# Layer norms by exp(-ln/2) and a rebuilt routed stage in a hybrid conv, attention and routed network: what it does to the time

## The chip, the cores and the metric

The kernel runs on one core of one Trainium2 chip. The metric is the device time of one launch in microseconds (us), the median of three runs. Besides the runs, one execution was taken with the hardware profiler; its trace holds every instruction with its start and length. Engines: PE is TensorE (PEld its weight loads), DVE is VectorE, ACT is ScalarE, SP is the queue that issues the DMAs. A name with q (SPq, DVEq) is the sequencer of an engine, which runs register loads, branches and waits.

## The reference

The input is 16 sequences of 256 positions with 32 channels, f32. Five blocks follow each other, each added to the residual `X`:

```python
# norm over the 32 channels ahead of each block: (x - mean) / sqrt(var + 1e-5)
# L0: recurrence over the 256 positions, state = tanh(A state + input), out = C state + D skip
# L1: group norm, three 1x1 projections with prelu, softmax(q k) v over positions
# L2: causal attention, 4 heads, rope, LoRA on q, k, v; then a linear, batch statistics and
#     a second recurrence over 256 positions, state = sigmoid(V state + input)
# L3: a two-direction Mamba-like scan (decays exp(segment sums), silu gates, RMS norm each way)
# last, a routed network: 33 blocks x 19 operations
op = argmax(h[0, 0, :19])               # of the first token, before the first step and after each
# block i acts if attn_mask[i, op] or ffn_mask[i, op]; ffn is relu(h w1 + b1) w2 + b2
```

A block that has neither mask set for the picked operation is skipped. With the given data the kernel before executes two feed-forward steps and no attention step of the routed network (the profile shows 2 sets of the feed-forward's DMAs and none of the attention's).

## The kernel before

Channels and a group of 4 sequences lie on the 128 partitions, 4 x 256 positions on the free axis, so a full tensor is 128 x 1024 and its halves 128 x 512 fill one PSUM bank each. Each engine has its own instruction list, written out by hand; they meet only in named semaphores (`then_inc`, `wait_ge`). An engine works strictly through its list. `link(...)` in DVE's list makes the next DVE instruction wait for this one.

A **norm** (`norm_tensor`, `norm_vector`, `norm_scalar`, used five times) runs so: PE multiplies by the centring matrix (L234, two halves); ACT squares (L270) and DVE copies the centred values (L253); PE sums squares with the data as the stationary side, so that a variance lies by token (L238, 8 small products); ACT takes the square root (L274), DVE the reciprocal (L257) and spreads it over 32 columns (L259); PE turns it back (L244, 8 products); DVE multiplies (L264). ACT loads the table of the square root ahead of each (L267).

The two **recurrences** (`recur_tensor`, `recur_scalar`) are 256 steps each, in which a small PE product (L314) and one ACT function (L332) wait for each other. The inputs of 32 steps lie in one PSUM bank; in the first recurrence DVE must add a bias to a bank (`bias_bank`, L1042) before step 32k of it can start. PE writes the input products of bank k+1 between steps 17 and 26 of bank k. Between `bias_bank(1)` and the loop that does `bias_bank(2)` DVE's list holds the making of the routing table `acting` (L1054 to L1060): for each of 33 blocks and 19 operations, the next block that acts. It is a chain of 33 pairs of linked 19-element operations.

The **Mamba block** has 48 units in each direction: exp on ACT (L985), a product on DVE (L1287), PE around them, and every 12 units a gate on DVE (L343, L346). In the second direction DVE also normalises the first one's result, one quarter every 12 units: a reciprocal of 128 x 256 (L1308), two short operations (L1309, L1310). At the end the same is done for the second direction in two halves of 128 x 512 (L1316, L1318, L1319).

The **routed stage** (`routed`) runs on all engines at once. Each engine has its own registers for the block and the operation; it loads the operation (L397, L419), then `acting` (L398, L421), then the two masks (L404, L405), and branches. In a feed-forward step SP issues four DMAs (L459 w1; L463 to L465 b1, w2, b2). w1 lies 4 times on the partitions; DVE spreads it into four matrices with zeros (`w1z`, L1375), PE multiplies (L837, 8 products of 128 rows), ACT and DVE take the relu in turn (L1017, L1390), PE the second layer on four column strips at once (L846), DVE adds the bias (L1381). Only then does `pick` read the first token out of the result for the next operation (L1329 to L1337). The three nested loops have 36 turns; those left over are run through as empty ones (L424). Then DVE adds `xn` to `X` (L1397) and SP stores it.

## Time and profile before

| what | value |
|---|---|
| median of 3 runs | 739.93 us (739.02 to 740.48) |
| the profiled execution's own time | 742.2 us |
| its span, first to last instruction | 740.4 us |
| two recurrences, first to last step | 27.4 to 157.9, and 362.4 to 506.0 |
| last norm finished, routed stage begins | 688.4 |
| routed stage, up to the last write of its result | 688.4 to 729.8 |
| loops left, last add and store | 729.8 to 740.4 |
| busy share of PE, DVE, ACT | 71%, 46%, 45% |

All times in the text are in us from the span's start, unless marked otherwise. In rows of the timeline the first number is the start, the second the busy time of the group, xN the number of instructions merged, and the bracket the engine's idle time before it with what ended it. An f32 product appears as two PE instructions.

### The profile page before, as it was taken

Reading aid. Unit: us, or ns where it says so; the run is one execution under the profiler, and the core shown is the slowest. Engines: PE = TensorE matmul, PEld = TensorE weight load, DVE = VectorE, ACT = ScalarE, POOL = GpSimd, SP = SyncE. Lnnn points to the kernel's source line nnn. Section 1 sums busy time; section 2 is a strip of 40 time slices with the busy share of each in tenths; the row PEclk is TensorE's granted clock in tenths of the full one; section 3 lists DMA queues with packets and bytes.
Section 4 is the critical chain, followed back from the end, with each engine's and each line's share of the span. In section 5 each row is a group of like instructions: output and inputs, shape, how many; then the busy total and the mean of one; then the engine's idle time right before and its main releaser. Section 6 shows DMA issues by size and latency. Waiting matters only on the chain. (4 is left out here: it accounts for less than half of the span.)

```text
span 740.4 us, 10964 instructions
## 1 busy us (share of the span) xinstructions
PE 526.8 (71%) x4080; PEld 302.9 (41%) x4081; DVE 337.7 (46%) x734; ACT 334.3 (45%) x1095; POOL 0.2 (0%) x4
## 2 busy tenths in 40 slices
PE   6656556557986899998566666667689998975463
PEld 5322222234655677665233333335245534542220
DVE  2161000038857788886600000002589946985233
ACT  2133333326737677775233333333455658643120
POOL 0000000000000000000000000000000000000000
PEclk9999999999998999999755555555699999997777
DMA  4000000000000000000000000000400000000000
GB/s 174 1 1 1 1 0 1 1 0 1 2 1 0 1 2 1 1 1 2 0 1 0 1 1 0 1 1 0 113 1 2 2 1 1 2 1 0 8 5 28
DMA packets 4954, 6.73 MB, mean 9 GB/s; under 512 B 1186, under 2 KB 4642, under 8 KB 4772
## 3 DMA queue, kind: packets, MB, share of 16 engines
q1 hardware_dynamic: 4900, 6.01, 2.6%
q8 instruction: 34, 0.56, 0.3%
q14 instruction: 20, 0.16, 0.1%
HBM read 3.38 MB, written 0.52 MB: 5 GB/s over the span
## 5 line engine op out<-in xcount | busy, mean ns | idle before, releaser
L314 PE MATMUL ps<-arena,wsb 16*16 16x16 f32 (+1 forms) x1024 | 131.0, 206 | 111.8 <-ACT arena L332 111.8
L332 ACT ACTIVATE arena<-ps 16x16 f32<-16x16 f32 (+1 forms) x512 | 96.3, 188 | 190.2 <-PE ps L314 190.2
L314 PEld LDWEIGHTS ps<-arena,wsb 16*16 16x16 f32 (+1 forms) x1024 | 76.1, 118 | 195.2 <-ACT arena L332 186.9
L338 DVE TENSOR_TENSOR X<-X,ps 128x128 f32<-128x128 f32 x16 | 4.6, 288 | 201.4 <-PE ps L297 201.4
L1287 DVE TENSOR_TENSOR arena<-arena,ps 128x512 f32<-128x512 f32 x96 | 61.2, 682 | 14.9 <-PE ps L740 5.6
L985 ACT ACTIVATE arena<-ps 128x512 f32<-128x512 f32 x96 | 54.1, 596 | 26.5 <-PE ps L728 13.0
L909 ACT ACTIVATE arena<-ps,arena 128x128 f32<-128x128 f32 (+1 forms) x128 | 52.4, 418 | 28.9 <-DVE arena L1160 28.8
L1159 DVE TENSOR_REDUCE arena<-ps 128x2 f32<-128x512 f32 (+1 forms) x48 | 33.0, 688 | 17.6 <-PE ps L580 10.3
L597 PE MATMUL ps<-wsb,arena 128*128 128x128 f32 x192 | 30.6, 283 | 11.2 <-DVE arena L1168 11.2
L762 PE MATMUL ps<-arena 128*32 128x128 f32 x768 | 31.4, 282 | 7.6 <-DVE arena L1287 7.5
L584 PE MATMUL ps<-arena 128*128 128x256 f32 x128 | 35.8, 404 | 0.0
L1168 DVE TENSOR_TENSOR arena<-arena 128x512 f32<-128x512 f32 x48 | 33.2, 692 | 1.6
L837 PE MATMUL ps<-xn,arena 128*128 128x512 f32 x32 | 19.5, 767 | 15.8 <-DVE arena L1375 15.8
L597 PEld LDWEIGHTS ps<-wsb,arena 128*128 128x128 f32 x192 | 22.2, 144 | 19.7 <-DVE arena L1168 17.8
L762 PEld LDWEIGHTS ps<-arena 128*32 128x32 f32 x768 | 18.3, 110 | 27.2 <-DVE arena L1287 19.0
L920 ACT ACTIVATE prob<-ps 128x512 f32<-128x512 f32 x48 | 28.8, 600 | 0.8 <-PE ps L597 0.8
L740 PE MATMUL ps<-arena 128*128 128x128 f32 x192 | 25.5, 276 | 3.3 <-DVE arena L1272 3.3
L740 PEld LDWEIGHTS ps<-arena 128*128 128x128 f32 x192 | 25.1, 192 | 6.5 <-DVE arena L1272 4.3
L1042 DVE TENSOR_SCALAR ps<-ps,u_b 16x512 f32<-16x512 f32 x8 | 6.0, 747 | 47.3 <-PE ps L292 47.2
L724 PE MATMUL ps<-csb 128*128 128x512 bf16 x64 | 24.6, 384 | 2.9 <-ACT arena L976 1.4
L584 PEld LDWEIGHTS ps<-arena 128*128 128x128 f32 x128 | 22.9, 200 | 8.0 <-ACT arena L909 5.8
L909 ACT ACTIVATION_READ_ACCUMULATOR arena<-ps,arena 128x1 f32 x128 | 25.6, 200 | 0.0
(231 smaller groups left out, 808.7 us busy)
## 6 DMA issues: line engine op xcount, KB each, us to landing
arena<-xn SPq DMA_DIRECT2D x16, 128.0 KB, 2.5
wsb<-weights SPq DMA_DIRECT2D x1, 1916.5 KB, 8.8
wsb<-weights SPq DMA_DIRECT2D x1, 549.5 KB, 4.8
X<-x SPq DMA_DIRECT2D x1, 512.0 KB, 3.9
out<-X SPq DMA_DIRECT2D x1, 512.0 KB, 3.0
csb<-consts SPq DMA_DIRECT2D x1, 160.0 KB, 8.7
arena<-w SPq DMA_DIRECT2D x2, 64.0 KB
arena<-b SPq DMA_DIRECT2D x4, 0.5 KB
```

Source lines behind the costliest of these rows:

```text
L314: nc.tensor.matmul(step_columns(k, rows, r), w_state, states[0:rows, :, :, t].rearrange("p g j -> p (g j)"), start=False, stop=True, skip_ ...
L332: nc.scalar.activation(states[0:rows, :, :, t + 1].rearrange("p g j -> p (g j)"), step_columns(t // STEP_BANK, rows, t % STEP_BANK), func) ...
L584: nc.tensor.matmul(bank[:, h * T:(h + 1) * T], q[:, j, P:T], kz[:, g * HEADS + 2 * (part - 1) + h, j, :], start=(h == 0), stop=False)
L597: mm = nc.tensor.matmul(ps[:, 3 + v % 3, i * P:(i + 1) * P], by_query[:, v % 3, i * P:(i + 1) * P], W("ident"), is_transpose=True, start=T ...
L740: mm = nc.tensor.matmul(ps[:, 4 + n // 4 % 2, i * P:(i + 1) * P], bz[:, one % G, one // G, sk * P:(sk + 1) * P], cpj[:, one // G, tq * P:( ...
L762: mm = nc.tensor.matmul(ps[rows, 6 + j % 2, c0:c0 + P], xdt[:, j * TT + st_, g, h, :], gram[:, (m + one) % 6, h * P:(h + 1) * P], start=(f ...
L909: ins = nc.scalar.activation(by_query[:, u % 3, h * width:(h + 1) * width], ps[:, u % 3, h * width:(h + 1) * width], ACT.Exp, bias=softmax ...
L920: nc.scalar.activation(prob6[:, v % 6, :], ps[:, 3 + v % 3, :], ACT.Copy).then_inc(s["L2 turned saved"], 1)
L985: nc.scalar.activation(decay[:, n % 3, :], ps[:, n % 4, :], ACT.Exp).then_inc(s["M decay"], 1)
L1159: link(nc.vector.reduce_max(softmax[:, u % 3, 0, 0:heads], ps[:, u % 3, :].rearrange("p (h k) -> p h k", h=heads), AX))
L1168: nc.vector.tensor_tensor(rows, rows, softmax[:, v % 3, 3, 0:heads].unsqueeze(2) .to_broadcast([P, heads, HALF // heads]), ALU.mult).then_ ...
L1287: nc.vector.tensor_tensor(gram[:, n % 6, :].rearrange("p (h t) -> p h t", h=HEADS), decay[:, n % 3, :].rearrange("p (h t) -> p h t", h=HEADS),
```

## The change

All five norms, the group norm, the batch statistics and the RMS norms take 1/sqrt(v) as exp(-0.5 ln v) on ACT, from one table set that holds both functions; the DVE reciprocals and most table loads go. A norm now sums the squares with one product by a block matrix for each half, which leaves the variance already on every channel. The routing table holds three words an entry (next block and both of its masks), so a step needs one register load instead of three. In the feed-forward step the weights come by two DMAs into one staging tile, from which DVE copies them; the four `w1z` matrices are gone, since each product takes only its 32 rows; the first token is put through both layers on its own first, and the next operation is picked from that; the result is stored in two halves.

```diff
 def norm_tensor(pe, n):
-                for jt in range(h * 4, h * 4 + 4):
-                    mm = nc.tensor.matmul(ps[:, 6 + h, jt * G:(jt + 1) * G], sq[:, jt * P:(jt + 1) * P], W("avg_by_group"),
...
-            (the same for "1/sigma rows" with W("ident"))
+                nc.tensor.matmul(ps[:, 6 + h, :], W("block"), halves(sq)[h], start=True, stop=True).then_inc(s["variance"], 1)
 def norm_vector(dve, n):
...
+                dve.wait_ge(s["1/sigma"], 2 * n + h + 1)
+                nc.vector.tensor_tensor(halves(xn)[h], halves(sq)[h], ps[:, h, :], ALU.mult).then_inc(s["normalised"], 1)
 def norm_scalar(act, n):
-            act.preload_act_table(ACT.Sqrt)
+            if n in (0, 3):
+                act.preload_act_table_set(EXP_LN)
...
+                nc.scalar.activation(halves(sq)[h], ps[:, 6 + h, :], ACT.Ln, bias=W("eps")).then_inc(s["log variance"], 1)
+                act.wait_ge(s["log variance"], 2 * n + h + 1)
+                nc.scalar.activation(halves(sq)[h], halves(sq)[h], ACT.Exp, scale=-0.5).then_inc(s["1/sigma"], 1)
 def routed(name, eng, attention, feed_forward, pick=None):
+            def look(to):
+                eng.wait_ge(s["op picked"], eng.snap(count[0]) + 1)
...
+                eng.reg_load(to, acting[0:1, bass.ds(entry * 3, 3)])
-                eng.reg_load(use_a, masks[0:1, 0, bass.ds(at_op, 1)])
-                eng.reg_load(use_f, masks[0:1, 1, bass.ds(at_op, 1)])
 SP feed_forward:
-                (w1s, then after "R ffn written": b1s, w2s, b2s)
+                sp.wait_ge(s["R weights taken"], n + 1)
+                sp.dma_start(arriving[:, 0:HID], w1[...].to_broadcast([G, C, HID])).then_inc(s["R weights"], 16)
+                sp.dma_start(arriving[:, HID:], w2_biases[...]).then_inc(s["R weights"], 16)
 PE feed_forward:
+                pe.wait_ge(s["R weights taken"], n + 2)
+                nc.tensor.matmul(ps[:, 7, 0:1], w1s[0:C, :], xn[0:C, 0:1], start=True, stop=True).then_inc(s["R first hidden"], 1)
+                pe.wait_ge(s["R first relu"], n + 1)
+                nc.tensor.matmul(ps[0:1, 7, P:P + C], token_hidden, w2s, start=True, stop=False)
+                nc.tensor.matmul(ps[0:1, 7, P:P + C], b2s, W("ident")[:, 0:C], start=False, stop=True).then_inc(s["R first out"], 1)
                 for k in range(2 * G):
-                    nc.tensor.matmul(ps[:, k % 4, :], w1z[:, k % G, :], halves(xn)[k // G], start=True, stop=True)\
+                    h, rows = k // G, slice(C * (k % G), C * (k % G) + C)
+                    if k == 2 * G - 1:
+                        pe.wait_ge(s["op picked"], step + 1)
+                    nc.tensor.matmul(ps[:, k, :], w1s[rows, :], halves(xn)[h][rows, :], start=True, stop=True)\
 ACT: Sqrt -> Ln, wait, Exp in "gn sigma", "F sigma", sigmas(d); 12 of 21 table loads gone
 DVE, making the table:
+            link(nc.vector.tensor_tensor(idle, tables[0], tables[1], ALU.max))
+            for i in range(NB):
+                nc.vector.tensor_scalar(following[:, i, :, 0], idle[:, i, :], float(i), None, ALU.mult)
...
             for i in reversed(range(NB)):
-                link(nc.vector.scalar_tensor_tensor(skipped[:], flags[:, i + 1, :], -float(i), flags[:, i, :], ALU.add, ALU.mult))
-                link(nc.vector.tensor_tensor(flags[:, i, :], flags[:, i + 1, :], skipped[:], ALU.subtract))
+                link(nc.vector.tensor_tensor(carried[:], following[:, i + 1], idle[:, i, :].unsqueeze(2).to_broadcast([1, NOPS, 3]), ALU.mult))
+                link(nc.vector.tensor_tensor(following[:, i], following[:, i], carried[:], ALU.add))
 DVE, Mamba block:
-                        link(nc.vector.reciprocal(oat[:, cols], oat[:, cols]))
-                link(nc.vector.reciprocal(halves(oat)[h], halves(oat)[h]))
 DVE feed_forward:
+                nc.vector.tensor_copy(expert, arriving).then_inc(s["R weights taken"], 1)
+                (max and max_index on the first token's row in PSUM; relu 1, 3, 5, 7; look(); out_half(0); out_half(1))
 DVE and SP, end: X + xn and the store in two halves
```

On DVE, in the making of the routing table behind `bias_bank(1)` (`skipped` and `carried` are the scratch rows, `prob` holds the table, `acting` its integer form), the kernel before has

```order
L1042 TENSOR_SCALAR ps<-ps,u_b 16x512
L1054 TENSOR_TENSOR acting<-masks 1x627
L1055 CAST prob<-acting 1x627
L1056 MEMSET prob 1x19
L1058 SCALAR_TENSOR_TENSOR skipped<-prob 1x19
L1059 TENSOR_TENSOR prob<-prob,skipped 1x19
```

and the changed kernel, in the same place,

```order
L1038 TENSOR_SCALAR ps<-ps,u_b 16x512
L1050 TENSOR_TENSOR prob<-arena 1x627
L1052 TENSOR_SCALAR prob<-prob 1x19 x33
L1054 CAST prob<-arena 1x627 x2
L1055 MEMSET prob 1x19x2
L1056 MEMSET prob 1x19
L1057 TENSOR_SCALAR prob<-prob 1x627
L1059 TENSOR_TENSOR carried<-prob 1x57
L1060 TENSOR_TENSOR prob<-prob,carried 1x57
```

The last two rows repeat 33 times in both; they now have 57 elements instead of 19, and 36 more instructions stand ahead of them. `bias_bank(2)` stands behind all of it in both.

On PE, in the feed-forward step of the routed stage (`ps` is PSUM, `arena` holds weights and hidden values), the kernel before has

```order
L836 ISA
L837 MATMUL ps<-xn,arena 128x512
L836 REGISTER_ALU
L837 MATMUL ps<-xn,arena 128x512
L836 REGISTER_ALU
L837 MATMUL ps<-xn,arena 128x512
L836 REGISTER_ALU
L837 MATMUL ps<-xn,arena 128x512 x3
L842 ISA
L846 MATMUL ps<-arena 32x512 x4
L837 MATMUL ps<-xn,arena 128x512 x2
L846 MATMUL ps<-arena 32x512 x4
```

and the changed kernel

```order
L823 MATMUL ps<-xn,arena 128x1
L824 REGISTER_ALU
L825 MATMUL ps<-arena 1x32
L826 MATMUL ps<-wsb,arena 1x32
L831 MATMUL ps<-xn,arena 128x512 x7
L830 REGISTER_ALU
L831 MATMUL ps<-xn,arena 128x512
L835 ISA
L837 MATMUL ps<-arena 32x512 x4
L835 REGISTER_ALU
L837 MATMUL ps<-arena 32x512 x4
```

Three small products for the first token stand ahead of the eight first-layer products, the last of which waits for the pick; the second layer comes behind all eight.

On DVE, in the same step, the kernel before has

```order
L1375 TENSOR_SCALAR arena<-arena,wsb 128x128 x4
L1377 ISA
L1389 ISA
L1390 TENSOR_SCALAR arena<-ps,arena 128x512
L1389 REGISTER_ALU
L1390 TENSOR_SCALAR arena<-ps,arena 128x512
L1389 REGISTER_ALU
L1390 TENSOR_SCALAR arena<-ps,arena 128x512
L1381 TENSOR_SCALAR xn<-ps,arena 128x512
L1387 ISA
L1329 STREAM_TRANSPOSE h<-xn 32x32
L1330 ISA
```

and the changed kernel

```order
L1371 COPY arena<-arena 128x162
L1372 REGISTER_ALU
L1374 MAX best<-ps 1x8
L1375 ISA
L1377 MAX_INDEX op_at<-best,ps 1x8
L1380 ISA
L1381 TENSOR_SCALAR arena<-ps,arena 128x512
...
L386 ISA
L388 TENSOR_LOAD op_at
...
L390 TENSOR_LOAD acting
L1386 TENSOR_SCALAR xn<-ps,arena 128x512 x2
```

The pick moves from behind the first half of the result to ahead of DVE's first relu (L1381), and the register loads (L386 to L390) to ahead of the two result writes (L1386).

## Rows read from the trace of the kernel before

**Rows 1.** The page, part 4: the chain that ended last, by line.

```profile
PE ps L837 2%; DVE arena L1287 1%; PE ps L762 1%; DVE oat L1316 1%; DVE oat L1308 1%; DMA arena<-w 1%; ACT arena L985 1%; PE ps L234 1%; PE ps L728 0%; PE ps L846 0%; DVE arena L343 0%; PE ps L740 0%; PE ps L724 0%; DVE xn L1381 0%; PE ps L244 0%
```

**Rows 2.** The timeline, first norm.

```profile
9.71 3.78 PE L234 MATMUL ps<-X,wsb 128*128 128x512 f32 x4
...
20.36 0.69 DVE L264 TENSOR_TENSOR xn<-xc,ps 128x512 f32<-128x512 f32 x1 [1.02 <-PE ps L244]
```

**Rows 3.** The timeline, second norm.

```profile
209.87 1.98 PE L234 MATMUL ps<-X,wsb 128*128 128x512 f32 x4 [0.81 <-DVE X L1125]
...
215.97 0.69 DVE L264 TENSOR_TENSOR xn<-xc,ps 128x512 f32<-128x512 f32 x1 [0.20 <-PE ps L244]
```

**Rows 4.** The timeline of DVE, routing table and the bank biases around it.

```profile
41.99 0.79 DVE L1054 TENSOR_TENSOR acting<-masks 1x627 int32<-1x627 int32 x1
...
43.46 0.17 DVE L1058 SCALAR_TENSOR_TENSOR skipped<-prob 1x19 f32<-1x19 f32 x1
...
56.70 0.49 DVE L1060 CAST acting<-prob 1x646 int32<-1x646 f32 x1
...
57.58 0.75 DVE L1042 TENSOR_SCALAR ps<-ps,u_b 16x512 f32<-16x512 f32 x1
```

**Rows 5.** The timeline of PE, the recurrence's step 64.

```profile
60.08 0.22 PE L314 MATMUL ps<-arena,wsb 16*16 16x16 f32 x2 [0.37 <-ACT arena L332]
```

**Rows 6.** The timeline behind the fourth norm.

```profile
518.74 10.52 SPq L447 DMA_DIRECT2D arena<-xn  x16
...
532.11 6.21 PE L644 MATMUL ps<-arena 128*64 128x512 f32 x16 [5.46 <-ACT arena L941]
```

**Rows 7.** The timeline of ACT and DVE, third unit of the second direction.

```profile
614.97 1.28 ACT L947 ACT_TABLE_LOAD   x1
...
616.26 1.34 ACT L947 ACTIVATE oat<-oat,wsb 128x512 f32<-128x512 f32 x2
...
619.59 3.68 DVE L1287 TENSOR_TENSOR arena<-arena,ps 128x512 f32<-128x512 f32 x6 [2.73 <-issue]
```

**Rows 8.** The timeline of DVE: two gates of each direction, a reciprocal.

```profile
579.00 0.74 DVE L343 SCALAR_TENSOR_TENSOR arena<-arena,wsb,ps 128x512 f32<-128x512 f32 x1
...
589.61 0.74 DVE L343 SCALAR_TENSOR_TENSOR arena<-arena,wsb,ps 128x512 f32<-128x512 f32 x1
...
623.19 1.75 DVE L1308 RECIPROCAL oat<-oat 128x256 f32<-128x256 f32 x1
...
632.64 0.74 DVE L343 SCALAR_TENSOR_TENSOR arena<-arena,wsb,ps 128x512 f32<-128x512 f32 x1
...
644.68 0.74 DVE L343 SCALAR_TENSOR_TENSOR arena<-arena,wsb,ps 128x512 f32<-128x512 f32 x1
```

**Rows 9.** The timeline, end of the Mamba block.

```profile
669.97 3.35 DVE L1316 RECIPROCAL oat<-oat 128x512 f32<-128x512 f32 x1 [3.52 <-ACT oat L947]
670.53 1.88 PE L662 MATMUL ps<-arena 128*64 128x512 f32 x8
...
678.79 0.69 DVE L1319 TENSOR_TENSOR X<-X,oat 128x512 f32<-128x512 f32 x1
```

**Rows 10.** The chain in order of time: a register load of SP, the first weights.

```profile
691.97 0.27 SPq L404
...
693.35 3.22 DMA arena<-w
```

**Rows 11.** The timeline of the routed stage.

```profile
697.48 7.21 PE L837 MATMUL ps<-xn,arena 128*128 128x512 f32 x12 [9.80 <-DVE arena L1375]
...
704.62 1.07 PE L846 MATMUL ps<-arena 128*32 128x512 f32 x8
...
729.04 0.75 DVE L1381 TENSOR_SCALAR xn<-ps,arena 128x512 f32<-128x512 f32 x1 [1.33 <-PE ps L846]
735.74 1.23 DVE L1397 TENSOR_TENSOR X<-X,xn 128x1024 f32<-128x1024 f32 x1 [5.94 <-issue]
```

**Rows 12.** Busy time of PE, PEld, DVE, ACT, POOL, then granted clock, DMA.

```profile
678.00:681.00 3.00, 1.47 (x2) 0.84 (x3) 1.41 (x3) 0.00 (x0) 0.00 (x0) 0.50 0.00 0
```

196 lines of the change are left out of this document (93 added, 103 removed).

## The prediction

> **What bounds the kernel now.** First the page: no engine is busy throughout, and its chain of waits is scattered over many lines with a per cent or two each [rows 1]. It is a program of latencies, and a term counts only where its wait ends last. So I read stage by stage in the timeline, then the chain in order of time for the last 125 us. The reader is to see that the two recurrences (130 and 144 us) are a ping-pong of PE and ACT that the change does not touch, and that what it does touch lies between them (norms), at the Mamba block's end (reciprocals of 3.35 us on DVE, with everything waiting), and in the routed stage, where SP, DVE and PE wait for each other in turn.
>
> Two rates of PE matter: four PE instructions of 512 columns take 3.78 in the first norm and 1.98 in the second [rows 2, 3], so an f32 product costs 1.71 at the half clock (1.2 GHz) and 0.86 at the full one. The profile's granted clock says 0.50 where the last norm begins, behind seven us in which PE did nothing [rows 12].
>
> **The change, part by part.** All in times of the profiled execution (span 740.4, own time 742.2, 0.3% over the median of 739.93); differences carry over to the median.
>
> *Norms.* Before, from PE's first instruction to the last write of `xn`: 11.34 in the first (9.71 to 21.05), 6.79 in the second (209.87 to 216.66) [rows 2, 3]. After, at full clock: the first half's variance is ready after three products and about 0.3, at 2.9; then Ln, Exp, Ln, Exp follow each other on ACT, each 0.67 (two ACT operations of 512 take 1.34 [rows 7]), to 5.6, and DVE's 0.69 ends at 6.25. That is 0.5 less. At half clock the second variance ends last: four products of 1.71 and 0.4 are 7.2, Ln, Exp and 0.69 make 9.3, so 2.0 less. The first and fourth norm run at the half clock: **-4.1** together. Second and third: -1.1 at best. But PE now idles some 2.8 in each of them, where before it was kept busy by the second transposing pass; if the clock falls there, the products behind them run at half rate for a while, which I price as two products of 0.86 extra behind the second and one behind the third: between -1.1 and +1.5. I take **0**.
>
> *Behind the fourth norm.* The load of a table between Exp and Ln of the time steps goes (1.28, the length of any load here [rows 7]). PE at 532.11 waited for ACT [rows 6], but the 16 shifted copies are issued until 529.26 and the last, issued at 528.6, lands 2.5 later by the page's part 6, at 531.1. So of 1.28 only about **-0.7** comes out before the DMA binds.
>
> *Routing table, in the first recurrence.* Here the change adds work to DVE, ahead of `bias_bank(2)`. Before: from 41.99 to 57.19, and the bias at 57.58 to 58.33 is 1.7 ahead of step 64 at 60.08 [rows 4, 5]. The 66 linked operations take (56.70 - 43.46)/66 = 0.201 each. An f32 operation with two inputs costs (0.79 - 0.17)/(627 - 19) = 1.02 ns an element [rows 4], so 57 elements make it 0.24: 66 x 0.04 = +2.6. The 33 new unlinked 19-element operations: at least 0.08 each (their length less what lies beside the next), at most 0.17: 2.6 to 5.6; I take 2.8, since unlinked ones overlap. One more cast (0.4 to 0.8), the flip of `idle` (0.5), a memset (0.1), and a last cast of 1938 instead of 646 elements (+0.7, at the rate of 0.49 for 646). Sum +7.0 (6.5 to 10). The cover is 1.7 and the gap from bias to step about 0.1, so the recurrence stops once for 7.0 - 1.7 = **+5.3** (4.6 to 8). Later banks are on time again: nothing is made up, as the steps are a pure ping-pong.
>
> *Square roots in the Mamba block.* In the third unit ACT loads a table, does two square roots, loads again: 3.9. After: four operations of 0.67, 2.7. **-1.2.** The Trainium skill prices a switch of tables higher, in "ScalarE: Activation LUTs", What ACT_TABLE_LOAD costs: 1283 ns and a drain of about 1380. By it two loads less would save 2.8 more here; the row shows the next ACTIVATE 0.01 behind the load [rows 7], so the measurement decides and I leave it out.
>
> *Quarter reciprocals (L1308, 1.75 each).* Twelve units take 12.04 in the second direction (632.64 to 644.68) and 10.61 in the first, which has gates but no reciprocals [rows 8]. So the floor set by the others is about 10.6 to 10.9 and a reciprocal is worth 1.2, not 1.75. The last stands ahead of the last three units with nothing beside it, full 1.75. Three of 1.2 and that: **-5.4** (-4.0 to -7.0).
>
> *Half reciprocals (L1316, 3.35 each).* DVE's tail was 669.97 to 679.48 [rows 9]. After: M out of the first half is there at about 671.5, of the second at 672.5; two operations of 0.7 each half end at 674.3. **-5.1**, -6.8 if PE, now idle 1.8 less, is still at full clock there. The last norm follows: 8.88 before, half clock at first. PE's rest ahead of it shrinks from 7.1 to 2.0, so it takes between 8.0 and 6.3; I take **-1.7** (-0.9 to -2.6).
>
> *Routed stage.* Step by step for the first feed-forward, times as if it began at 688.41 as before. SP drops two loads with their index arithmetic (0.27 for one load alone [rows 10]), 0.9: first DMA at 692.5, second 1.0 later. Data is usable 3.22 after issue [rows 10]: 696.7 (2.5 would make it 696.0). Copy 0.2, token product, ACT, two products 0.45 + 0.3 + 0.6 (PE instructions of one column in the first microseconds of the kernel are of this size): 698.3; max and index 0.7: the operation is known at **699.0**, where before it came behind the first half of the result, itself behind the second layer of 704.62 [rows 11]. The eight first-layer products start at 698.2. Four column strips at once took 1.07 for four products [rows 11]; if four row strips do the same, they are two rounds of 1.71: 701.7, against 9.1 for 8 products before (7.21 for the first six [rows 11]). The relus end at 703.2. Second layer to 704.4 or, at half clock, 705.5; DVE looks up the next block meanwhile and writes both halves by 706.3. SP has long had the pick, and the weights lie in the staging tile at 706.3. Loop and branches of DVE and PE, about 2.2, start the second step at 708.6; 9.5 as before: it ends at **718.1** instead of 729.79 [rows 11]. The loops left took 5.95 until the add at 735.74; without the look (two loads of 0.3 and arithmetic, 1.3) 4.65. Halved add: the second half's ends at 724.1, before 736.97. **-12.9**, and -0.1 for half the store lying ahead. Range -10 to -15, since no wait on registers of the new order is shown.
>
> The skill's page "TensorE: Matmul & The Clock Gate", Measured speedup vs the span model, has 3.07 for four row strips. By it each round is 0.5 longer and the stage 2 us longer.
>
> *At no cost:* the group norm's and the batch statistics' extra Exp replaces a reciprocal of equal length, 0.2; the other table loads lay beside DVE or PE work; the masks in the arena change no wait.
>
> **Sum.** -4.1 + 0 - 0.7 + 5.3 - 1.2 - 5.4 - 5.1 - 1.7 - 13.0 = -25.9. **740 - 26 = 714.**
>
> **Rivals.**
> - *The row strips run one after the other.* No row shows row strips beside each other: where this kernel uses 32-row operands it waits between them. For it: f32 products of two instructions each, in order. Against: the column strips overlap. Then each step takes 5.2 longer: **724.5**. Chance 0.12.
> - *The recurrence does not stop.* If the unlinked operations and casts cost next to nothing and wider rows nothing, +1.7 stays covered: **709**. The margin is exceeded by the wider rows alone, so 0.04.
> - *The PE clock falls at each new rest and costs in the attention stage too*: +1.5 above my zero, and about 3 more (two more rests of four products at 0.86 extra, by halves) in its first units: **718.5**. Chance 0.14.
> - *Slower than before: another route.* Ln and Exp round differently from square root and reciprocal. If the first token's two largest values lie that close, another operation is picked, and for seven of the 19 operations blocks 1 to 7 run with attention too. A feed-forward step alone costs about 12 after the change, so more than two extra steps lose the 26, and seven would give **over 800**. Nothing in the profile speaks for so close a pick. Chance 0.02.
> - My forecast, 0.68: own range 708 to 720.
>
> **How the numbers follow.** The bounds of the sum: low, -1.1 for the norms, -1.6 for the quarters, -1.7 and -0.9 at the end, -2 in the routed stage, not all at once: 707. High, +1.5, +2.7, +1.4, +0.8, +3 likewise: 720; the serial strips take it to 725, of which I keep 723. Range **707 to 723**. No change is told from a measurement of this kernel within 0.2%, 1.5 us; only the other route, or table work of over 30 us, gets there: faster 0.97, same 0.01, slower 0.02.
>
> **What would show it.** After: step 64 of the first recurrence follows a PE rest of over 5, released by DVE's `bias_bank`; 12 units of the second direction in 10.6 to 10.9; the last norm within 8; eight first-layer products in under 4 at half clock, starts in groups of four; 10 from one step's weights to the next. Wrong if the strips' starts are 0.86 apart, if DVE's 57-element rows take other than 0.24, or if the weights' second DMA lands much later than 3.2 after issue.

## The result

The changed kernel takes **714.18 us** (median of four runs, 709.43 to 715.27) against 740.2 for the kernel before beside it (739.02 to 741.01): a ratio of 0.964, 95% interval 0.960 to 0.967. The prediction was 714, 707 to 723. The profiled execution has a span of 712.2 (own time 713.98), the one of before 740.4: 28.2 less, where the medians differ by 26.0 and the sum said 25.9.

A caution before the terms are compared. Later runs of the kernel before lay between 736.7 and 745.4, and every kernel below spreads over 2 to 8 us, so the 0.2% that I took for what a measurement can tell was too fine. Of 44 later runs of the kernel before, 15 are of the sort from which both of its profiles come (mean granted clock given as 0.84 to 0.85 instead of 0.74 to 0.75), with a median of 742.5 against 740.6 for the others. The first of these profiles is of a run of 742.2, which is why the profiles differ by more than the medians. The last section says where the spread sits. A term is therefore read in the trace, between two checkpoints, and not from medians; and where a second profile of the kernel before gives another length than the first, the text says so.

First the page of the changed kernel, the granted clock in 40 slices and the chain by line. The reader is to see that no line of DVE has taken the place of the reciprocals, which stand in [rows 1]. The two lines can't be compared further: the chain of the kernel before, from which the prediction started, adds up to 16% of its span and reaches back only to about 616, so it said nothing of the recurrences. This one covers the whole span, and the recurrence's two lines hold 26%.

```profile
span 712.2 us, 10651 instructions
...
PEclk9555555556899899999965555555589999999876
...
PE ps L295 16%; ACT arena L313 10%; PE ps L273 4%; PE ps L278 3%; PE ps L753 3%; PE ps L731 3%; PE ps L588 2%; PE ps L719 2%; PE ps L575 2%; PE ps L235 2%; PE ps L571 2%; PE ps L715 2%; PE ps L602 2%; DVE arena L1159 2%; DVE arena L1168 2%
```

The same checkpoints in both traces (ends and starts of the norms, first and last step of the recurrences, first Exp and last gate of the Mamba block's second direction) cut the span into pieces:

| piece | before | after | difference | term of the prediction |
|---|---|---|---|---|
| start, first norm, on to the recurrence | 27.67 | 24.76 | -2.9 | -2.05 |
| first recurrence | 130.08 | 135.05 | +5.0 | +5.3 |
| attention blocks up to the second norm | 52.12 | 52.50 | +0.4 | 0 |
| second and third norm | 13.72 | 12.56 | -1.2 | } 0 together |
| stage between them | 129.80 | 130.52 | +0.7 | } |
| second recurrence, with what leads to it and from it | 153.92 | 154.05 | +0.1 | 0 |
| fourth norm | 11.34 | 8.41 | -2.9 | -2.05 |
| to PE's L635 (before L644) | 13.46 | 12.97 | -0.5 | -0.7 |
| from there to the second direction's first Exp | 80.86 | 80.07 | -0.8 | 0 |
| to its last gate | 52.01 | 46.64 | -5.4 | -1.2 - 5.4 |
| to the last X | 14.5 | 9.5 | -5.0 | -5.1 |
| last norm | 8.87 | 7.88 | -1.0 | -1.7 |
| routed stage and store | 51.95 | 37.25 | -14.7 | -13.0 |

Now the rows of the changed kernel for the larger terms. The timeline of its first norm on PE, then ACT, then DVE, against [rows 2]: the last variance instructions already run faster (four in 3.13 instead of 3.78). The first variance is there at 15.0, the second at 16.25, just ahead of the second half's Ln, which starts at 16.33 right behind the first half's Exp; so it is ACT's four operations, back to back, that end last.

```profile
9.54 3.78 PE L235 MATMUL ps<-X,wsb 128*128 128x512 f32 x4
13.12 3.13 PE L238 MATMUL ps<-sq,wsb 128*128 128x512 f32 x4
...
15.07 0.69 ACT L253 ACTIVATE sq<-ps,wsb 128x512 f32<-128x512 f32 x1 [1.11 <-PE ps L238]
15.79 0.63 ACT L255 ACTIVATE sq<-sq 128x512 f32<-128x512 f32 x1
16.33 0.67 ACT L253 ACTIVATE sq<-ps,wsb 128x512 f32<-128x512 f32 x1
17.03 0.63 ACT L255 ACTIVATE sq<-sq 128x512 f32<-128x512 f32 x1
...
17.69 0.69 DVE L243 TENSOR_TENSOR xn<-sq,ps 128x512 f32<-128x512 f32 x1 [0.55 <-ACT sq L255]
```

The routing table's end on DVE and PE's step 64, against [rows 4, 5]: the last pair starts at 59.56, the cast of 1938 elements takes 1.16, the bias comes behind it, and PE rests 5.45, of which 0.37 is the rest of any step.

```profile
59.81 0.21 DVE L1060 TENSOR_TENSOR prob<-prob,carried 1x57 f32<-1x57 f32 x1
60.05 1.16 DVE L1061 CAST acting<-prob 1x1938 int32<-1x1938 f32 x1
61.24 0.29 DVE L319 TENSOR_TENSOR X<-X,ps 128x128 f32<-128x128 f32 x1
61.45 0.74 DVE L1038 TENSOR_SCALAR ps<-ps,u_b 16x512 f32<-16x512 f32 x1
...
62.24 0.23 PE L295 MATMUL ps<-arena,wsb 16*16 16x16 f32 x2 [5.45 <-DVE ps L1038]
```

The end of the Mamba block, against [rows 9]. DVE now waits for PE's product (5.25), and not ACT and PE for DVE:

```profile
659.72 2.72 PE L653 MATMUL ps<-arena,wsb 128*64 128x512 f32 x8 [2.28 <-ACT arena L948]
...
662.22 2.85 PE L653 MATMUL ps<-arena 128*64 128x512 f32 x8
...
664.26 0.69 DVE L1315 TENSOR_TENSOR oat<-oat,ps 128x512 f32<-128x512 f32 x1 [5.25 <-PE ps L653]
...
666.30 0.69 DVE L1316 TENSOR_TENSOR X<-X,oat 128x512 f32<-128x512 f32 x1
```

The routed stage, chain in order of time, against [rows 10, 11]. Sixteen instructions of first-layer products take 3.40 and 3.73, the second layer is issued while DVE looks up the next block, and DVE's look holds a load of 0.77.

```profile
677.07 0.70 SPq L383
...
679.65 0.73 SPq L452
...
680.66 2.88 DMA arena<-w_biases
683.57 0.26 DVE arena L1371
...
684.06 0.59 PE ps L823 x2
...
685.36 3.40 PE ps L831 x16
...
689.98 0.77 DVEq L390
690.79 1.47 DVE xn L1386 x2
...
694.43 0.26 DVE arena L1371
...
695.94 3.73 PE ps L831 x16
699.67 3.00 PE ps L837 x16
702.69 0.76 DVE xn L1386
...
708.10 0.69 DVE X L1401
```

### The profile page after: what moved, and what is told of

It reads as the page before. It is cut to its first block, busy times and chain, and to the rows that moved or that the text cites. A ratio compares the mean times of both kernels' runs of the same rounds, so it can differ in the third digit from the quotient of the medians.

```text
span 712.2 us, 10651 instructions
## 1 busy us (share of the span) xinstructions
PE 497.7 (70%) x3952; PEld 276.9 (39%) x3953; DVE 315.8 (44%) x723; ACT 331.1 (46%) x1101; POOL 0.2 (0%) x4
## 4 chain that ended last, share of the span: by engine, by line
PE 57%; DVE 16%; ACT 16%; issue 7%; SPq 2%; DMA 1%; DVEq 1%
PE ps L295 16%; ACT arena L313 10%; PE ps L273 4%; PE ps L278 3%; PE ps L753 3%; PE ps L731 3%; PE ps L588 2%; PE ps L719 2%; PE ps L575 2%; PE ps L235 2%; PE ps L571 2%; PE ps L715 2%; PE ps L602 2%; DVE arena L1159 2%; DVE arena L1168 2%
## 5 line engine op out<-in xcount | busy, mean ns | idle before, releaser
L273 PE MATMUL ps<-xn,wsb 32*32 32x128 f32 x64 | 20.0, 414 | 2.8 <-DVE xn L1204 2.6
```

The lines of the kernel that those rows point to most:

```text
L273: nc.tensor.matmul(ps[0:rows, k, g * P:(g + 1) * P], w_in[group, C * g:C * g + rows], xnj[group, :, STEP_BANK * k:STEP_BANK * (k + 1)], st ...
```

## The experiments

Times are medians of four to ten runs, but for the second look at the kernel before. The kernel before ran beside them at 740.2 to 740.9.

| kernel | time (range) | profiled span |
|---|---|---|
| changed kernel | 714.18 (709.4 to 715.3) | 712.2 |
| table in pieces | 709.35 (706.7 to 711.9) | 710.1 |
| packed table | 712.81 (711.6 to 713.9) | 710.9 |
| quarter reciprocals back | 716.17 (714.2 to 719.6) | 717.8 |
| half reciprocals back | 718.48 (717.6 to 720.2) | 716.7 |
| one row strip | 736.52 (733.8 to 740.6) | 731.9 |
| pick from the result | 718.68 (718.0 to 721.6) | 716.2 |
| PE kept busy in the wait | 719.78 (715.8 to 721.4) | 713.9 |
| before, with the norms alone | 735.80 (733.7 to 738.9) | 731.9 |
| before, once more | 739.21 (one run) | 737.4 |
| no attention branch | 713.24 (711.7 to 716.6) | 712.1 |
| second norm filled | 711.59 (709.3 to 712.4) | 709.6 |
| table in pieces, norm filled | 705.53 (702.3 to 710.5) | 708.7 |

### 1. Is the stall in the recurrence the table's, and nothing else?

```
+            blocks = list(reversed(range(NB)))
             for k in range(BANKS):
                 if k > 0:
                     add_bank_out(dve, 0, k - 1)
                 if 0 < k < BANKS - 1:
                     bias_bank(k + 1)
+                if k < 4:
+                    carry(blocks[9 * k:9 * k + 9])     # the 33 pairs, in pieces; the loop over all of them goes
+                if k == 4:
+                    link(nc.vector.tensor_copy(acting[:], ...))
```

> The changed kernel, with the 33 pairs of the routing table's carry made in four pieces of up to nine, behind the bias of banks 2, 3 and 4 instead of all ahead of bank 2. Same instructions, same number. My theory (the recurrence of the changed kernel is longer because PE's step 64 waits for DVE's bias of bank 2, 5.45 us of rest in its profile, and for nothing else): the recurrence lasts 130.5 again and not 135.5, the rest at step 64 is gone, the span falls from 712.2 to about 707.1, the time from 714.2 to about 709. Rival A (the recurrence is slower in the changed kernel for another reason: PE's granted clock stands at 0.50 there and stood at 1.00 before): it stays at 135, time 714. Rival B (a piece of nine pairs, 4.4 us, comes up against the next bank's bias too): each of three banks takes up to 4.4 back, time between 709 and 722.

The first nine pairs still stand ahead of bank 2's bias; 24 pairs and the cast have gone behind it. The recurrence lasts 130.17 (130.08 before, 135.05 in the changed kernel). The waits of PE between 24 and 70 us, longest last, hold no wait for DVE any more; the changed kernel's stand below them:

```profile
PE ps L295 <- ACT arena L313: 19.9, 71, 0.4
```

```profile
PE ps L295 <- ACT arena L313: 17.3, 62, 0.4
PE ps L295 <- DVE ps L1038: 5.4, 1, 5.4
```

The time is 4.8 below the changed kernel's. Rivals A and B are out: no later bank waits, and PE's granted clock is 0.50 throughout this recurrence as in the changed kernel's, which lasts 5 longer. (The 1.00 that rival A names for the kernel before can't be trusted: its profile gives 1.00 between 9.7 and 20 too, where four instructions take 3.78 [rows 2], the length at the half clock.) The second profile of the kernel before has 130.25.

This profile also shows something that I had not looked for. Its routed stage takes 40.83 where all the others that leave that stage alone take 37.2 to 37.9. Here is PE's timeline at the turn of the loop, and the instruction queue's packets between 686 and 693:

```profile
684.27 1.07 PE L837 MATMUL ps<-arena 128*32 128x512 f32 x8 [0.62 <-DVE arena L1387]
692.57 0.58 PE L823 MATMUL ps<-xn,arena 32*128 32x1 f32 x2 [7.23 <-issue]
```

```profile
q8 instruction: 3, 0.05, 4.0%
```

DVE had copied the weights by 688.65; PE comes 3.9 later, waiting for nothing that the profile shows. Instruction packets of 16 KB arrive in that stretch, at 687.6 and 688.8, and one more as PE starts. Between 688 and 696 the changed kernel has no such packet. That PE waited for them is a guess; the second of them is there 3.7 ahead of its start. PE's code is the same in both kernels, and the last kernel, which has this edit too, is at 37.6, so this belongs to a run, not to the edit.

### 2. Narrow rows and one word

```
-            eng.reg_load([at, use_a, use_f], acting[0:1, bass.ds(... * 3, 3)])
+            eng.reg_load(word, acting[0:1, bass.ds(..., 1)])
+            eng.reg_alu(at, word, 2, ALU.logical_shift_right)
+            eng.reg_alu(use_a, word, 1, ALU.bitwise_and)
+            eng.reg_alu(use_f, word, 2, ALU.bitwise_and)
```

> The changed kernel, with block and the two masks packed in one word (4 x block + 2 x ffn + attention), so that the table's rows are 19 elements wide again and the registers get one word, split by three register operations. Theory of the table: 66 linked operations at 0.20 instead of 0.24 give -2.7, the last cast of 646 instead of 1938 elements -0.6, the rest about even; of the 5.1 that the recurrence stops, about 1.5 to 2.0 stays. Theory of the routed stage: the load of three words took 0.70 to 0.77 in the changed kernel's profile where a load of one takes about 0.28, so each of three loads on the chain is 0.45 shorter, less three register operations of unknown price (at most 0.1 each by what lies between the loads): -0.4 to -1.3. Sum: span 707.5 to 708.5, time about 710. Rival (the long load is the second of two that follow each other, and a load of one word is as long there): the load stays at 0.7, the stage gets 0.3 longer for each split: time 711.5.

Waits of PE between 24 and 70 us: the one for DVE is 2.8 instead of 5.4, and the recurrence 132.35 instead of 135.05.

```profile
PE ps L295 <- DVE ps L1043: 2.8, 1, 2.8
```

So width is half of the stall. What is left (2.3) is of the size of the 33 unlinked operations, which take 2.67 in both kernels, as priced (2.8); no run takes them away alone. (The packing also puts two linked operations of 627 elements in the place of two casts.) The load of one word takes 0.30 in the chain where three words took 0.70 (both at SP's entry):

```profile
675.62 0.30 SPq L388
```

But the way from the last `xn` to SP's first DMA is 4.52 instead of 4.72: the three register operations give half of it back, and the routed stage stays at 37.41. Half the theory holds, that on the table; the routed stage gains nothing that can be told, and the time is 1.4 lower where about 4 were expected.

### 3. The reciprocals, put back one kind at a time

```
-  nc.scalar.activation(halves(oat)[h], halves(oat)[h], ACT.Exp, scale=-0.5)
+  nc.scalar.activation(halves(oat)[h], halves(oat)[h], ACT.Exp, scale=0.5 if d == 0 else -0.5)
...
+                        link(nc.vector.reciprocal(oat[:, cols], oat[:, cols]))
```

> The changed kernel, with the forward half's deviation made as Exp(+Ln/2) and DVE's four reciprocals of 256 columns (1.75 each) back ahead of the four quarter updates. Nothing else. Theory by the changed kernel's profile (PE is busy through 11.07 of 11.07 us of each period of 12 units, so PE is the floor, and the first period, 12.11 with or without, is PE's too): +0 for the first, +0.97 for two, +2.2 for the last, 4.1 in all: time 718.3. Rival A (my prediction's sizes: floor 10.6 to 10.9): +5.4 and more, 719.6. Rival B (each is on the path with its full length): +7.0, 721.2.

From the first Exp to the last gate: 51.14 against 46.64, so +4.5. From a reciprocal to the next 12.11, 12.39 and 12.04 (12.11, 11.07 and 11.08 in the changed kernel between the same places), and 5.68 instead of 3.46 behind the last. The first costs nothing, exactly as the profile said: PE is busy throughout that period either way. Busy times of a later period, changed kernel and kernel before, PE first:

```profile
631.92:642.99 11.07, 11.07 (x141) 6.63 (x140) 9.69 (x17) 7.25 (x15) 0.00 (x0) 1.00 0.01 2
```

```profile
635.23:647.26 12.03, 11.20 (x141) 6.62 (x140) 11.21 (x18) 7.35 (x15) 0.00 (x0) 1.00 0.01 2
```

The theory's 4.1 holds in the trace. The median moved by 2.0 only, with four runs spread over five us; by it alone the theory could not be told from rival A.

With the halves, DVE's two reciprocals of 3.35 are back at the end, nothing else:

```
                 dve.wait_ge(s["M sigma"], 2 + h + 1)
+                link(nc.vector.reciprocal(halves(oat)[h], halves(oat)[h]))
```

> The changed kernel, with the backward half's deviation made as Exp(+Ln/2) and DVE's two reciprocals of 512 columns (3.35 each) back at the end of the Mamba block. Theory (the last product of the output, 664.2 in the changed kernel, hides 2.0 of the first; the second lies bare): the last X at +4.9; and PE then rests seven us again ahead of the last norm, which takes 8.9 instead of 8.0. Sum +5.8: time 720. Rival A (the norm behind it doesn't depend on how long PE rested): +4.9, 719.1. Rival B (the last norm and the routed stage both start at the lower clock and take 2 more in the first-layer products): +7.5, 721.7.

From the last Square on ACT, behind the last gate, to the last X 12.76 against 7.95: +4.8. PE then rests 6.78 ahead of the last norm and starts it at the lower clock; it takes 8.84 (7.88 after a rest of 1.98). Together 5.8 as expected, 4.3 in the time.

### 4. One row strip instead of four

```
-                    h, rows = k // G, slice(C * (k % G), C * (k % G) + C)
+                    h, rows = k // G, slice(0, C)
```

> The changed kernel, with all eight first-layer products of the routed step on the same row strip, that of strip 0, so that they can't run beside each other. Left out by it: the results of the images in strips 1 to 3 come from strip 0; the token that decides, and the route, are the same. Theory (four row strips run at once: 16 instructions took 3.40 and 3.73 in the changed kernel): one product after the other costs 0.86 to 1.71 each by the clock, so 8 take 9 to 13 instead of 3.4 to 3.8; 1.4 of that hides the relus; each of the two steps gets 4.5 to 8 longer: time 723 to 730. Rival (16 instructions are that short for another reason, such as the 32 rows): no change, 714.

Timeline of PE, and busy times of that stretch with the clock:

```profile
682.71 14.02 PE L831 MATMUL ps<-xn,arena 32*128 32x512 f32 x16
```

```profile
682.70:696.70 14.00, 14.00 (x22) 5.18 (x22) 2.67 (x6) 2.76 (x4) 0.00 (x0) 0.50 0.03 6
```

The same 16 instructions take 14.02 on one strip and 3.40 to 3.80 on four: four at once, with next to nothing lost. Each step is 10.6 longer in its products, the stage 60.18 instead of 37.25, the time 22.3 more. That is above the range that I gave (723 to 730). Its upper end already had 13 for the eight products, nearly the half clock, but took 1.4 off for relus hidden beside them; the lower end let the clock rise as it did for the 128-row products of before (six in 7.21 [rows 11]). Neither came: the clock stayed at 0.50 through 14 us of 32-row products, and each step is 11.5 longer in all.

### 5. The deciding token first

```
-                nc.tensor.matmul(ps[:, 7, 0:1], w1s[0:C, :], xn[0:C, 0:1], ...)     # and its second layer
...
+                out_half(0)
+                dve.wait_ge(s["R ffn written"], n * 2 + 1)
+                pick(step)
                 look()
-                out_half(0)
                 out_half(1)
```

> The changed kernel without the products of the deciding token: the next operation is picked from the first half of the result, as in the kernel before; the rest (two DMAs into the staging tile, row strips, words) stays. Theory (SP's 3.5 from the pick to its first DMA and 3.9 to the data are hidden only if the pick comes early): each step starts its products 1.3 earlier; the pick, 1.0 on DVE, comes behind the first half's write, so the second step's weights are there 4.9 later than in the changed kernel; the end has 1.0 of pick more ahead of the look. Sum -2.6 + 4.9 + 1.0 = +3.3: time 717.5. Rival (the 3.9 of the second step's weights are hidden beside DVE's second half, loop and branches anyway): -0.6, time 713.6.

The stage takes 42.65 instead of 37.25: +5.4, in the time +4.5. First products to second step's: 14.58 against 10.58, and DVE waits 4.0 for the weights of the second step:

```profile
690.52 0.06 DVE L1326 MEMSET h<- 1x1 f32 x1
692.49 0.75 DVE L1372 TENSOR_SCALAR xn<-ps,arena 128x512 f32<-128x512 f32 x1 [1.91 <-issue]
697.26 0.25 DVE L1363 COPY arena<-arena 128x162 f32<-128x162 f32 x1 [4.02 <-DMA arena<-w_biases]
```

The theory holds in kind, and its 3.3 was too low: I had left out that the look (1.9) now also stands ahead of the second half.

### 6. Would PE be faster if it did not rest? And when is it there at all?

```
+                for k in range(3):
+                    nc.tensor.matmul(ps[:, 6, :], W("ident"), halves(X)[0], start=True, stop=True)
                 pe.wait_ge(s["R weights taken"], n + 2)
```

> The changed kernel, with three f32 products of 512 columns, whose result nothing reads, issued by PE ahead of its wait for the routed weights in each step. Theory (in the changed kernel the granted clock is at half during 5.5 of the 7.1 us of first-layer products and in all of the second step's second layer, because PE rested before): with PE busy in the wait the clock is full there; step one 1.2 less, step two 1.9 + 1.0 less, against 0.5 by which the third product may be late: -2.5 to -4, time 711. Rival (the clock does not follow so little work, or falls again in the rests between): +0.5 for each step, 715.

Timeline of PE:

```profile
679.36 5.48 PE L823 MATMUL ps<-X,wsb 128*128 128x512 f32 x6 [12.27 <-issue]
...
685.71 2.00 PE L833 MATMUL ps<-xn,arena 32*128 32x512 f32 x16
...
693.81 4.37 PE L823 MATMUL ps<-X,wsb 128*128 128x512 f32 x6 [2.96 <-issue]
```

The clock part of the theory is right: behind them the 16 instructions take 2.00 instead of 3.40 to 3.80. The rest is wrong, and it is what the run taught. There is no free time for them: PE starts the first of them 9.8 us behind the last `xn`, when DVE has already copied the weights (by 9.4 here), and comes round the loop 3.0 after its last product, at 693.81, when DVE's copy is 0.1 away. So all three products lie bare in both steps. The stage is 44.34, 7.1 longer; the time 5.6 more.

What keeps PE was asked by leaving the attention branch out:

```
-                with eng.If_ne(use_a, 0):
-                    attention(i, o, eng.snap(count[1]))
-                    eng.reg_add(count[1], count[1], 1)
```

> The changed kernel without the routed stage's attention branch on every engine: no test of its mask and none of its code. Left out by it: the attention of routed steps, which the route of these inputs never takes, so that the same work is done. Theory (PE reaches the first step's code 8.0 to 8.7 after the pick because it jumps over the attention's code and has to load what lies behind it: with the three extra products it started at 8.7, and two 16 KB packets of the instruction queue run in that time): PE is ready earlier, but the weights land 7.5 after the pick anyway, so the first step gains 0.3 at most on PE, each step 0.3 to 0.5 on SP and DVE for the test of the mask that goes; the stage lasts 36 to 36.7 instead of 37.25, the time is about 713. Rival (all engines' way through the routed code is set by fetching it): SP's first DMA comes more than 1 earlier and the stage lasts under 35: time under 712.

One 16 KB packet of the instruction queue instead of three in that stretch; PE's first product 0.05 behind DVE's copy instead of 0.24, and the weights' last DMA takes 2.02 instead of 2.88. Chain in order of time:

```profile
680.50 0.75 SPq L449
...
681.53 2.02 DMA arena<-w_biases
683.57 0.26 DVE arena L1368
683.88 0.60 PE ps L820 x2
```

PE is there 7.9 behind the last `xn`, where the changed kernel has its first product at 9.1, but it waits for the weights either way. Stage 36.11 against 37.25, the time 0.9 less, which is inside the spread. The rival is out: the first DMA comes 0.2 earlier, not 1. The theory's size came out by luck: 0.86 of the 1.14 is the shorter DMA, for which it had no part. That DMA takes 2.88 in the packed kernel too and 2.29 and 2.50 in two others; whether instruction packets beside it make the difference was not tried by itself.

### 7. The norms alone, and what their rest costs

The kernel before, with the new norm functions and nothing else:

```
-                for jt in range(h * 4, h * 4 + 4):
-                    mm = nc.tensor.matmul(ps[:, 6 + h, jt * G:(jt + 1) * G], sq[...], W("avg_by_group"), ...)
+                nc.tensor.matmul(ps[:, 6 + h, :], W("block"), halves(sq)[h], start=True, stop=True)
```

> The kernel before with nothing but the new norms (one product for each half's variance, Ln and Exp on ACT, one operation on DVE), the table of Ln and Exp loaded at each of the five. Theory by the five profiles of the changed kernel and its variants: first norm -2.5 to -3.2, second -0.5, third -0.6, fourth -2.9, fifth 0 to -1, since PE rests 7 us ahead of it as before; and PE's rest of 2.6 in the second norm gives 0.7 to 2.5 back in the stage behind it (129.8 before, 130.5 to 132.4 in the profiles of the changed kernel): sum -5 to -7, time 735. Rival A (my prediction's terms, each norm at its own clock, nothing given back): -4.1, 736.8. Rival B (the longer stage behind the second norm has nothing to do with the norm): it lasts 129.8 here, sum -7.5, time 733.

Time 735.80: -4.9 beside its own 740.7. In pieces: norms 7.98, 6.28, 6.28, 8.45 and 8.09 (-3.4, -0.5, -0.6, -2.9, -0.8), and the stage behind the second 132.08 instead of 129.80: +2.3 given back. The way from the fourth norm to PE's time steps is 0.7 shorter too (12.78 instead of 13.46): the norm has left the table of Ln and Exp in ACT, and the two loads that stood there go without any other edit. Rival B is out; rival A's 736.8 is inside the spread of the medians, and only the pieces speak against it. (The profiled run, 8.4 below that of before, is its fastest; 1.5 of that is the way from the first norm to the recurrence, 5.10 instead of 6.62, at a clock that rose earlier.) The head of that stage, this kernel and then the kernel before:

```profile
211.54 3.57 PE L534 MATMUL ps<-xn,wqkv 128*128 128x512 f32 x4 [2.63 <-DVE xn L243]
```

```profile
216.81 1.96 PE L554 MATMUL ps<-xn,wqkv 128*128 128x512 f32 x4 [0.87 <-DVE xn L264]
```

Behind a rest of 2.63 the first products run at half rate, behind one of 0.87 they don't. It does not happen each time: in the changed kernel's own profile the same four take 1.95. Of ten profiles with the new norm as it is, six have the late head (the ninth instruction 5.3 behind `xn`) and four have not (3.65). The same happens behind the third norm, where PE's rest is 2.54 instead of 0.78: in three of twelve profiles with the new norm (the pick from the result, no attention branch, and the last kernel below) the first four instructions take 3.5 to 3.7 instead of 1.98, and the stretch from the third norm to the fourth is 155.4 to 155.7 instead of 154.0.

> The kernel before once more, for a second profile of it. Asked: does the stage between the second and the third norm (129.81 in its first profile) and the way from the first norm to the recurrence (6.62) vary from run to run in the old kernel too? Theory (PE's rest of 2.6 in the new second norm lets the clock fall at the head of that stage): 129.8 here again, within 0.3. Rival (the stage has run-to-run states of its own in both kernels): anything from 129.8 to 132.4.

The stage is 129.70 here, so this is no state of the old kernel. But two other pieces differ from its first profile with nothing changed: the fourth norm takes 9.18 instead of 11.34, because its sixteen variance instructions took 1.91 instead of 3.41, and the last 8.62 instead of 8.87. Span 737.4 instead of 740.4.

Then two products that nothing reads, in the second norm's rest:

```
+            if n == 1:
+                for k in range(2):
+                    nc.tensor.matmul(ps[:, 4, :], W("block"), halves(X)[k], start=True, stop=True)
```

> The changed kernel, with two f32 products of 512 columns, whose result nothing reads, behind the variance products of the second norm alone, where PE otherwise rests 2.6 until xn is written. Theory (that rest lets the granted clock fall at the head of the next stage in some runs: 130.5 to 132.4 in eight profiles, against 129.8 in the kernel before): rest 0.9, the stage lasts 130.6 or less, time 0 to 1.5 less than the changed kernel's, 713.5. Rival A (the clock falls there whether PE rests 0.9 or 2.6): 132.3 as often as before. Rival B (the products end late and hold up the first projection): stage 0.5 longer.

The rest is 0.92, the ninth instruction comes at 3.66, the stage is 130.66: as where the clock did not fall. Time 711.59, 2.6 under the changed kernel, a little more than was to be had.

### 8. Both

> The changed kernel with the table's carry in four pieces behind banks 2 to 4 and the two filling products in the second norm, together. Theory: the recurrence lasts 130.2 (as with the pieces alone), the first eight products behind the second norm take 3.65 in every run and not 5.35 as in six of eleven profiles of kernels with the new norm; the time is that of the pieces alone, 709.4, less 0 to 1.7: 708.5. Rival (the fall of the clock behind the second norm does not care for PE's rest there): 5.35 again in about half of the runs, 709.4.

**705.53** (ratio 0.952, 0.949 to 0.955): 8.7 under the changed kernel and the fastest of all. Timeline of PE behind the second norm, then behind the third:

```profile
210.29 1.88 PE L241 MATMUL ps<-X,wsb 128*128 128x512 f32 x4
213.09 1.96 PE L548 MATMUL ps<-xn,wqkv 128*128 128x512 f32 x4 [0.92 <-DVE xn L246]
...
348.98 3.46 PE L618 MATMUL ps<-xn,wsb 128*128 128x512 f32 x4 [2.54 <-DVE xn L246]
```

The ninth instruction at 3.66, the stage 129.70, the recurrence 129.90. PE's rest ahead of the last line, in the third norm, is not filled: there the clock fell in this profile. The table's pieces are shown to be worth 5. That the filling products hold the clock is not settled: two profiles of two have the short head, where four of ten had it without them, and by chance alone that comes out one time in six. The medians (-2.6 and -3.8 for the filling) speak for it, inside overlapping ranges. The profiled run is the slowest of the six (710.5; the others 702.3 to 706.9), so its trace does not show why the median is lower than the 708.5 expected; that stays open.

## Why the prediction was right, point by point

- **Norms, -4.1 for the first and fourth.** Right in mechanism, too small: -2.5 and -2.9. The step that was off is "at half clock the second variance ends last": the clock rises during the variance products (3.13 and 2.35 for four, where I had two times 1.71), so ACT's chain ends last. In the fourth norm, though, three quarters of the 2.9 are in the choice of profile: the kernel before has 9.18 in its second one, 0.8 above the changed kernel's 8.41.
- **Second and third norm, 0.** The mechanisms were both there: -0.5 and -0.6, and the clock fell at the new rest in six profiles of ten. Then the stage is 132.1 to 132.4 or, with the later falls at other places, 131.5; without it 130.5 to 130.7. I had priced two products of 0.86, 1.7, behind the second norm, and 1.7 is what a fall costs there; behind the third I had 0.86, and the fall that came in three profiles of twelve costs 1.4 to 1.7. The changed kernel's own profile has neither fall: it has -1.2 in the norms and +0.7 in the stage, for another reason than the one priced. The stages of 130.5 to 130.7 have two later falls of the granted clock, those of 129.7 (the kernel before twice, and the last kernel) have three; why, I cannot say.
- **Behind the fourth norm, -0.7.** -0.5 here and -0.7 to -0.8 in the other kernels with the new norm. The -0.8 behind it was in no term: PE's 16 instructions of L635 take 5.43 instead of 6.21 [rows 6], at a clock that rose earlier. The second profile of the kernel before has 5.67, so most of this is the choice of profile again.
- **Routing table, +5.3.** +5.0, with the parts as priced: pairs at 0.24, unlinked 2.67, cast 1.16 instead of 0.49. Experiment 1 removes it, experiment 2 halves it. This was the cost of the change, and it could have been had for nothing.
- **Square roots, -1.2, no drain.** DVE begins the first quarter's work 8.92 behind the first Exp instead of 10.22. The rule of the Trainium skill in "ScalarE: Activation LUTs", What ACT_TABLE_LOAD costs (a drain of about 1380 ns beside the load) would by my estimate have given 2.8 more; this case's trace does not agree.
- **Quarter reciprocals, -5.4.** -4.2 by the trace and 4.5 put back. The mis-sized step is "the floor set by the others is about 10.6 to 10.9", taken from the first direction: in the second PE has eight instructions more in a period and is the floor at 11.07, and in the first period at 12.11. For the last one the full 1.75 was too low in turn: 2.2. The sign "12 units of the second direction in 10.6 to 10.9" failed with it.
- **Half reciprocals, -5.1.** -5.0, and 4.8 put back. The end of the block is now PE's, at half clock (eight instructions of the last product in 2.85, against 1.88 in [rows 9]).
- **Last norm, -1.7.** -1.0 in this profile; of the profiles with the short rest ahead of it four have 7.88 and six 6.28, where PE was at full clock from its first product. My bound of -2.6 is that state.
- **Routed stage, -13.0.** -14.7. First DMA at 4.7 behind the last `xn` instead of 4.1, since a load of three words takes 0.70 and not 0.28; copy at 8.6 instead of 8.3; from there each part is a little shorter than priced: out halves at 17.3 instead of 17.9, second copy 19.5 instead of 20.2, second step's end 28.5 instead of 29.7, exit 4.65 as said, add and store 0.5 shorter. Row strips, "two rounds of 1.71": close (3.73 for both at half clock, instead of 3.42). The rule that I cited from "TensorE: Matmul & The Clock Gate", Measured speedup vs the span model (3.07 for four strips), would by my estimate have put 0.5 on each round; 14.02 on one strip against 3.80 on four, both by the timeline and at half clock, is a factor of 3.7, so the trace does not agree with the rule here.
- **The rivals.** Serial strips would have cost 22, not the 10.5 that I gave them (by the prediction's own 1.71 a product, eight against two rounds are 10.3 in each step, not 5.2), and they didn't come. The recurrence did stop. The clock's fall did come, but not in all runs, and elsewhere the clock rose earlier than in the kernel before. No other route was taken: two feed-forward steps, as before.

So the mechanisms were right but for the floor in the Mamba block and the end of the first and fourth norm, and 714 came out with errors of both signs; that the medians differ by 26.0 where the sum has 25.9 is luck. In the profile, below the sum: 0.9 in each of first and fourth norm, 1.2 in second and third, 1.7 in the routed stage, 0.8 behind the fourth norm, 0.3 in the table. Above it: 1.2 in the Mamba block's second direction, 1.1 in the two attention stages, 0.7 in the last norm, 0.4 in small ones. The last kernels say what the change left lying: 5 us of a table built ahead of a bias that PE waits for.

## What to carry to other kernels

Work that "has time until much later" should be put behind the operations for which another engine waits, in pieces, even where its engine looks idle: 5 us went for widening 33 pairs of tiny operations and putting 33 more ahead of them. When a stall is removed, count what the next engine is busy in that very stretch, and not in a neighbour that looks alike: the floor there was 11.07 and not 10.6. And before an empty wait of PE is filled with work, ask whether PE has arrived: in this routed stage a rest shown as "issue" behind a branch was not free time.

## What the runs showed of the hardware

- One kernel's runs differ by up to 9 us of 740, and the profiles show several of the places: at places at which PE's granted clock changes, the same instructions take one of two lengths. Four instructions 1.95 or 3.65 behind the second norm; the last norm 6.28 or 7.88; the fourth norm of the kernel before 9.18 or 11.34. With them go longer stretches: from the third to the fourth norm 154.0 or 155.4 to 155.7, from the first recurrence to the second norm 51.0 to 52.5. The recurrences repeat to 0.4 us and the Mamba block's gates to 0.02 us in kernels with the same code there.
- The clock stayed at 0.50 through 14 us of unbroken 32-row products on one strip, while it rose to 1.00 during the 128-row products of the changed kernel's first norm (four in 3.13 instead of 3.78), and in experiment 6 behind the filling ones (the 16 next instructions in 2.00).
- Four row strips of f32 products with 512 columns run at once: 16 instructions in 3.73 to 3.80 at half clock, 2.00 at full, against 14.02 on one strip at half clock.
- A register load of three words takes 0.70 to 0.77, of one word 0.28 to 0.30; at SP's entry three register operations gave back 0.2 of the 0.4 that the packed word had saved.
- A branch over unused code goes with instruction packets of 16 KB: three ahead of the first routed step, one without the branch. Once, in one profile of eleven with this loop as it is or nearly, they came at the turn of the loop, and the stage was 3.6 us longer; that the packets were the cause is not shown.
